# Two-phase convolution for three of the four channel groups, with the constant products at a tile's end taken out, in a fused attention, router and state-space kernel

## The chip, the cores and the metric

One core of a Trainium2 chip runs the whole program. The metric is the device time of one launch in microseconds (us).

## What is computed

The input x has 8 sequences of 512 tokens with 256 numbers each. Four layers run one after the other, each on the layer-normed x and added to it; the reference, cut to what matters here:

```python
x = x + attention(layernorm(x))            # linear attention, 16 heads
x = x + experts(layernorm(x))              # 8 experts, the best one for each token
x = x + state_space(layernorm(x))          # the layer that is changed
x = x + experts(layernorm(x))

# state_space; d_inner 512, d_state 16, 4 taps
xc, z = split(x @ in_proj_w.T)
h = conv(pad(xc, 3 in front), conv_w)      # 512 x 512 channels, 4 taps, causal
u = h + conv_b
dt = clip(sigmoid(u @ dt_w.T + dt_b), 1e-4, 1.0)
Bm, Cm = u @ B_w.T, u @ C_w.T
state = exp(clip(dt * A)) * state + dt * Bm * u + 1e-6    # per token, 16 states per channel
y = sum(state * Cm) + D * u
out = (y * silu(z)) @ out_w.T
```

## The kernel before

All arithmetic is fp32. Each engine has its own program, written out by hand; semaphores join them. The 8 sequences are called tiles here (`b`, or `n` for the one that is prepared).

**The state-space layer** holds over half of the time. It runs 8 tiles, each of 64 slots (`q`): 16 states by 4 groups of 128 channels. In a slot TensorE turns four 128x128 pieces of the scan's input into PSUM (`m_spread`, L1645ff, recorded under the helper's L1300), ScalarE makes the decay (`m_decay`, L745) and a quarter of the input of the next state (`m_input`, L755), and VectorE runs one scan over 512 tokens (`m_scan`, L1197). After four slots GpSimd multiplies the state's four scans by C (`c_product`, L500) and issues a DMA that adds the product to one of two sums (`add_on`, L509). C comes as one broadcast DMA per state from SyncE's queue (L396), two ahead.

**Beside the scans of tile b the next tile is prepared**, and the last one closed. Tables at the top say in which slot each instruction is issued on TensorE (`CONV_AT`, `UT_AT`, `BC_AT`, `DT_AT`, `DTT_AT`, `Z_AT`, `OUT_AT`, `XT_AT`), on ScalarE (`UC_AT`, `UTC_AT`, `TH_AT`, `ZTH_AT`, `XTC_AT`, `SKIP_AT`) and on VectorE (`ADD_AT`, `FINAL_AT`, `UPDATE_AT`, `STAT_AT`, `CLIP_AT`, `WT_AT`, `GATE_AT`). TensorE may be at most three slots ahead of the scans (three PSUM banks), and it does in order what stands in a slot.

**The convolution** (`m_conv`, L1556ff, products at L1567) has the input projection already folded into its taps (`tap`, L1443ff: `tapw[k]` = in_proj times conv tap k, eight products of four parts, L1449, copied out at L618). For each of 4 output groups `o` it adds up 4 taps by 2 halves of the input: 8 products of 128x128 weights by 512 tokens, so 32 a tile. An fp32 product has two matmul records in the trace, a transpose one. `m_uevac` (L699) copies it out and adds the bias, then come the transposes of u (L1575), the B and C product (L1584) and the dt products (L1598).

**In slots 59, 61 and 62** of each of the first seven tiles TensorE also computes a product of constants that nothing reads (`m_spin`, L1695 to L1699, `SPIN_AT`).

**The rows x** of the first four tiles stay in SBUF from the layer's start; the place of the other four holds two of the seven state buffers, and their rows come again from memory in tiles 2 to 5 (`ld_again`, L403 to L409). Rows of a finished tile go out (`store_rows`), and in the last tile four tiles' rows come back into `staged` for the next router (L416 to L425).

**The first expert layer** begins with the router: TensorE turns x and makes logits (`x_turn`, `logits`), VectorE makes the tables (`feed`, L992ff), GpSimd gathers the rows. TensorE's `feed` places tap product 0 before the counting products L1464 and L1466, 1 and 2 behind them, 3 behind the sorting products L1475; 4 to 7 follow the experts. The tap weights are loaded by SyncE after all rows are stored (L367 to L376).

**Before the first scan** tile 0 is prepared with nothing beside it: TensorE L1725 to L1748, ScalarE norms, copies, three decays and the four input pieces of state 0, VectorE row statistics of all rows, then clips (L1121) and weights (L1134) in the slot order of the tables.

```python
            for o in range(KI):
                for i in range(TAPS * KD):
                    m_conv(0, o, i)
                    if o and i == TAPS:
                        m_uturn(0, o - 1)
                        m_bcmm(0, o - 1)
```

Of the kernel before, what the change touches and what calls it, by code (L numbers as in the profile page):

```python
# [17 lines left out]
P = 128  # L18
BATCH, SEQ, D = 8, 512, 256
TOK = BATCH * SEQ  # L20
NCH = TOK // P
# [12 lines left out]
PAD = TAPS - 1  # L34
LN_EPS, NORM_EPS = 1e-5, 1e-6
# [15 lines left out]
CONV_AT = ((0, 1, 2, 2, 3, 4, 5, 6), (7, 8, 8, 10, 11, 12, 13, 14), (14, 15, 16, 17, 18, 20, 21, 21), (22, 23, 24, 26, 28, 29, 30, 30))  # L51
UT_AT = (12, 19, 25, 34)
OUT_AT = ((23, 25, 25, 26, 28, 29, 32, 33), (38, 39, 41, 43, 43, 47, 49, 49))
BC_AT = (19, 23, 27, 34)
DT_AT = ((33, 34, 36, 36), (37, 38, 39, 40), (43, 44, 45, 47), (48, 49, 50, 51))
DTT_AT = (40, 44, 50, 55)
BT_AT = 41
C_STORE = 10
SPIN_AT = (59, 61, 62)
Z_AT = ((52, 53), (54, 55), (56, 57), (58, 59))  # L60
XT_AT = (52, 53, 55, 57)

# [12 lines left out]
UPDATE_AT = (34, 50)
STAT_AT = (36, 38, 58, 63)
SKIP_AT = (3, 5, 8, 16)
CLIP_AT = (38, 42, 48, 52)
WT_AT = (40, 45, 51, 56)
BTC_AT = 44  # L80
GATE_AT = (55, 57, 59, 61)


XT_BANK, CONV_BANK, UT_BANK, OUT_BANK = (0, 7), (0, 1, 0, 1), (0, 1, 0, 1), (4, 5)
BC_BANK, BT_BANK, DT_BANK, DTT_BANK, Z_BANK, Y_BANK = 7, 7, (0, 1, 0, 1), (0, 1, 0, 1), (4, 5, 4, 5), (4, 5, 7, 4)
SCAN_BANK = (2, 3, 6)
DT_FIRST = (2, 3, 4, 5)

# [55 lines left out]
def build(nc, T):  # L144
    with ExitStack() as ctx:
# [42 lines left out]
        class Space:  # L188
# [5 lines left out]
            def take(self, n):  # L194
# [31 lines left out]
        zero_row = s.take(ROW)  # L226

# [43 lines left out]
                for c in (RING * CPB, (RING + 2) * CPB)]  # L271
        m_c = [s.take(SEQ) for _ in range(RC)]
# [6 lines left out]
                  for w in (m_dt[0].rearrange("p k t -> p (k t)"), u_raw[0]) for i in range(2)]  # L279
        x_turned = ([f_xt[i % 2] for i in range(BATCH)], [halves[i // IN_LAST][i % 2] for i in range(BATCH)])  # L280
# [13 lines left out]
        def kept(b):  # L294

            return CPB * (b % RING)
# [9 lines left out]
        def z_bank(b, o):  # L306
            return ps[(Z_LAST if b == BATCH - 1 else Z_BANK)[o]]

# [16 lines left out]
        def _(sp):  # L325
# [44 lines left out]
            def send_tap(k):  # L370
                if k >= 2:
                    sp.wait_ge(S("tap_mm"), KD * (k - 1))
                sp.dma_start(cw[k % 2], T["conv"][k].rearrange("(k p) d -> p k d", p=P)).then_inc(S(f"ld_cw{k}"), 16)

            for k in range(TAPS - 1):
                send_tap(k)  # L376
# [1460 lines left out]
```

## Time and profile before

| | |
|---|---|
| median of 3 runs | 1475.5 us (1467.76, 1475.50, 1475.68) |
| the profiled execution | 1471.08 us, span 1469.3 us |
| attention and first router, up to the experts | about 0 to 242 us |
| first experts, up to the first preparation | about 242 to 408 us |
| preparation of tile 0 | about 408 to 472 us |
| the 8 tiles of scans | 472.3 to 1263.0 us |
| second router and experts | to 1469.3 us |
| mean granted TensorE clock | 0.978 of full speed |

A duration of a matmul record overlaps the next one's: what one costs in a dense run is the run's length over its count. A row of the timeline merges neighbours of one kind; its bracket is the idle time of that engine before it and what ended it. In a table by stretches each engine's column is its busy time, then the count of records; the clock is the share of full speed, 1.00 being 2.4 GHz and 0.50 being 1.2 GHz.

### The profile page before, as it was taken

How to read it: one execution, taken by the hardware profiler on the slowest of the kernel's cores; microseconds unless marked ns; L12 is line 12 of the kernel's file. 1: busy time of each engine (PE TensorE's matmuls, PEld its weight loads, DVE VectorE, ACT ScalarE, POOL GpSimd, SP SyncE). 2: the span in 40 equal slices, each digit the busy share in tenths (PEclk: the TensorE clock that was granted, in tenths of full speed). 3: DMA queues.
4: the chain of work that ended last, by engine and by line, in shares of the span. 5: the costliest groups of instructions: out<-in, count | busy, mean ns of one | idle time of the engine just before them, and what ended most of it. 6: DMA issues, size and time to landing. Idle time of an engine off the chain costs nothing.

```text
span 1469.3 us, 22230 instructions
## 1 busy us (share of the span) xinstructions
PE 1366.5 (93%) x7040; PEld 949.6 (65%) x7040; DVE 1011.8 (69%) x1529; ACT 937.7 (64%) x1737; POOL 861.1 (59%) x436
## 2 busy tenths in 40 slices
PE   5899998999998999999999999999999887979997
PEld 2566686999744555565655655655656576569996
DVE  6666634333332899899899898998998988853332
ACT  1222231344314999899999998999999999214442
POOL 1111002555200899798898897998988979225552
PEclk9999989999998999999999999999999979999999
DMA  9200044777420598898997997988979979376662
GB/s 301 85 29 29 19 98 144 211 206 210 153 65 16 118 219 195 179 221 186 201 222 181 205 220 176 218 190 193 223 170 204 230 195 234 79 235 203 208 210 82
DMA packets 108229, 248.39 MB, mean 169 GB/s; under 512 B 19097, under 2 KB 49950, under 8 KB 94048
## 3 DMA queue, kind: packets, MB, share of 16 engines
q0 software_dynamic: 23104, 131.96, 41.5%
q1 hardware_dynamic: 82944, 113.68, 25.6%
q10 hardware_dynamic: 2080, 1.47, 0.3%
q8 instruction: 55, 0.90, 0.2%
q14 instruction: 46, 0.38, 0.1%
HBM read 116.72 MB, written 18.94 MB: 92 GB/s over the span
## 4 chain that ended last, share of the span: by engine, by line
PE 67%; ACT 16%; DVE 10%; issue 4%; DMA 1%; another core or an unknown queue 1%; SPq 0%; DVEq 0%; ACTq 0%; POOLq 0%; POOL 0%
PE ps L1300 11%; PE ps L1513 9%; PE ps L1504 9%; PE ps L1567 7%; ACT arena L745 7%; PE ps L1598 7%; ACT arena L755 7%; PE ps L1325 4%; PE ps L1640 3%; PE ps L1629 3%; DVE arena L1197 3%; PE ps L1362 2%; PE ps L1584 2%; PE ps L1316 2%; PE ps L1449 1%
## 5 line engine op out<-in xcount | busy, mean ns | idle before, releaser
L500 POOL TENSOR_TENSOR arena<-arena 128x2048 f32<-128x2048 f32 x91 | 425.1, 4684 | 118.6 <-DVE arena L1197 117.4
L1300 PEld LDWEIGHTS ps<-cst,arena 128*128 128x128 f32 x2428 | 295.3, 143 | 280.1 <-issue 187.7
L1197 DVE TENSOR_TENSOR_SCAN arena<-arena,ps 128x512 f32<-128x512 f32 x364 | 431.7, 1209 | 62.3 <-PE ps L1300 58.7
L1300 PE MATMUL ps<-cst,arena 128*128 128x128 f32 x2428 | 365.7, 278 | 51.2 <-ACT arena L755 24.3
L745 ACT ACTIVATE arena<-arena,a_neg 128x512 f32<-128x512 f32 x512 | 365.9, 715 | 43.3 <-DVE arena L1197 29.6
L755 ACT ACTIVATE arena<-arena,m_bt 128x512 f32<-128x512 f32 x512 | 362.9, 709 | 3.8 <-DVE arena L1134 2.2
L1567 PE MATMUL ps<-arena,tapw 128*128 128x512 f32 x512 | 255.1, 600 | 0.7 <-ACT arena L693 0.7
L1197 DVE TENSOR_TENSOR_SCAN x<-arena,ps 128x512 f32<-128x512 f32 x148 | 175.7, 1209 | 21.9 <-PE ps L1300 20.6
L500 POOL TENSOR_TENSOR x<-x,arena 128x2048 f32<-128x2048 f32 x36 | 169.8, 4728 | 14.7 <-DVE x L1197 12.7
L1078 DVE TENSOR_TENSOR arena<-ps,arena 128x256 f32<-128x256 f32 x78 | 33.1, 425 | 205.7 <-PE ps L1513 131.4
L456 POOL DMA_INDIRECT arena<-rows,arena x78 | 75.9, 973 | 158.1 <-DVE arena L1058 134.9
L1504 PEld LDWEIGHTS ps<-arena 128*128 128x128 f32 x1248 | 154.7, 196 | 3.8
L1504 PE MATMUL ps<-arena 128*128 128x128 f32 x1248 | 154.9, 279 | 0.0
L1513 PE MATMUL ps<-arena 128*128 x624 | 147.5, 380 | 3.3 <-ACT arena L644 3.3
L637 ACT ACTIVATE arena<-ps 128x256 f32<-128x256 f32 x78 | 30.0, 385 | 157.8 <-PE ps L1300 156.5
L1598 PE MATMUL ps<-arena,dtw 128*128 128x512 f32 x256 | 128.6, 597 | 0.6 <-ACT arena L699 0.6
L1513 PEld LDWEIGHTS ps<-arena 128*128 128x128 f32 x624 | 112.5, 190 | 16.0 <-issue 3.7
L644 ACT ACTIVATE arena<-ps,b1t 128x128 f32<-128x128 f32 x312 | 89.3, 370 | 43.8 <-issue 29.5
L1567 PEld LDWEIGHTS ps<-arena,tapw 128*128 128x128 f32 x512 | 85.1, 193 | 36.1 <-issue 33.7
L447 POOL TENSOR_TENSOR x<-x,arena 128x1024 f32 (+1 forms) x8 | 18.9, 2358 | 120.0 <-DVE arena L868 114.4
L471 POOL DMA_INDIRECT residual<-arena x39 | 39.4, 1011 | 68.4 <-DVE arena L1085 67.2
L471 POOL DMA_INDIRECT out_x<-arena x39 | 39.3, 1008 | 67.5 <-DVE arena L1085 67.5
(164 smaller groups left out, 1573.0 us busy)
## 6 DMA issues: line engine op xcount, KB each, us to landing
arena<-arena POOLq DMA_DIRECT2D x52, 1024.0 KB, 8.3
arena<-in_W SPq DMA_DIRECT2D x94, 512.0 KB, 8.2
arena<-c_rows SPq DMA_DIRECT2D x128, 256.0 KB, 3.7
arena<-x POOLq DMA_DIRECT2D x28, 1024.0 KB, 8.4
x<-arena POOLq DMA_DIRECT2D x24, 1024.0 KB, 8.3
rows<-x SPq DMA_DIRECT2D x16, 512.0 KB, 4.2
x<-residual SPq DMA_DIRECT2D x12, 512.0 KB, 5.9
x<-in_x SPq DMA_DIRECT2D x8, 512.0 KB, 11.2
```

The costliest lines, as they stand in the source:

```text
L456: g.indirect_dma_start(out=t_x[j % XB], out_offset=None, in_=xs[r], in_offset=bass.IndirectOffsetOnAxis(ap=idx[:, j:j + 1], axis=0))\
L471: g.indirect_dma_start(out=x_mid if r == 0 else T["out"].rearrange("b s d -> (b s) d"), out_offset=bass.IndirectOffsetOnAxis(ap=idx[:, j:j ...
L500: g.tensor_tensor(h, h, m_c[i % RC].unsqueeze(1).to_broadcast([P, KI, SEQ]), ALU.mult)\
L644: last = a.activation(t_ht[par][:, k, :], ps[4 + par][:, k * P:(k + 1) * P], ACT.Relu, bias=b1t[:, row(e), k:k + 1].rearrange("p a b -> p ...
L745: a.activation(m_a[g % RA], m_dt[b % 2][:, k, :], ACT.Exp, scale=a_neg[:, k, n:n + 1])\
L755: a.activation(m_dbt[i % 2][:, c, :], m_wt[b % 2][:, c, :], ACT.Copy, bias=1e-6, scale=m_bt[b % 2][:, c, n:n + 1]).then_inc(S("m_dbt"), 1)
L1197: v.tensor_tensor_scan(out=h[:, k, :], data0=m_a[g % RA], data1=ps[SCAN_BANK[g % 3]][:, :], initial=0.0, op0=ALU.mult, op1=ALU.add).then_i ...
L1300: return t.transpose(bank, src[:, k * P:(k + 1) * P], ident)
L1504: last = t.matmul(ps[4 + par][:, h * P:(h + 1) * P], t_w1[j % WR][:, k, h * P:(h + 1) * P], t_xt[par][:, k, :], start=(k == 0), stop=(k == ...
L1513: last = t.matmul(ps[6 + par][:, 0:D], t_ht[par][:, k, :], w2[:, row(e), k, :].rearrange("p a h -> p (a h)"), start=(k == 0), stop=(k == K ...
L1567: mm = t.matmul(ps[CONV_BANK[o]][:, :], tapw[:, k, d, o * P:(o + 1) * P], m_xt[n % 2][:, d, k:k + SEQ], start=(i == 0), stop=(i == TAPS * ...
L1598: mm = t.matmul(dt_bank(n, o)[:, :], dtw[:, k, o * P:(o + 1) * P], m_u[n % 2][:, k, :], start=(k == 0), stop=(k == KI - 1))
```

## The change

**The convolution in two phases.** Even and odd tokens are computed together, from products over half the tokens each, with three quarters of the columns of before. Phase one (part 0) multiplies sums of two neighbouring taps (`tap_sum`, `sum_first`) with every second token: four products of 256 tokens, in one half of a shared bank (`BOTH_BANK`). ScalarE adds the bias and writes them into every second column of u (`m_both`). Phase two (parts 1 and 2) multiplies single taps with differences of neighbouring tokens (`m_xd`, `xd_first`): eight products of 256 or 255 tokens. VectorE adds both (`m_join`). GpSimd makes the sums of taps once and the two differences once a tile (`m_differ`, after product 15). Groups 1 to 3 of tiles 1 to 7 are done so, and all four groups of tile 0; group 0 of the others stays as it was. All slot tables are changed.

**The constant products** `m_spin` and `SPIN_AT` are gone.

**Rows.** `m_xd` and `tap_sum` take the place of rows in SBUF, so rows of each tile are loaded twice: for its norm (at n == 8) and for its update (at n == 2); at the end of tile 6 three loads stand together. The rows of tiles 4 and 5 come back into the taps' place.

**Before the first scan** clips and weights are in another order, VectorE makes two of the four input pieces of state 0, and two norms and turns of tile 1 come earlier. **In the first router** the tap weights are loaded at the program's start, tap product 0 stands between the logits, 1 before the counting products, 2 behind them and 3 between the sorting products.

```diff
-CONV_AT = ((0, 1, 2, 2, 3, 4, 5, 6), (7, 8, 8, 10, 11, 12, 13, 14), ...
-SPIN_AT = (59, 61, 62)
+CONV_AT = ((0, 1, 1, 2, 3, 4, 5, 6), (5, 6, 7, 7, 9, 9, 10, 10, 11, 11, 12, 13), ...
+JOIN_AT = (15, 20, 24)
...
+                    if n == N_LOAD and b < BATCH - 2:
+                        sp.wait_ge(S("m_umm"), conv_done(b + 1, KI - 1))
+                        if b:
+                            sp.wait_ge(S("ld_rows"), 16 * b)
+                        sp.dma_start(x[:, CPB:2 * CPB, :],
...
+            def m_differ(n):
+                g.wait_ge(S("m_xtc"), KD * (n + 1))
+                for s in range(2):
+                    g.tensor_tensor((m_xd if n else xd_first)[:, s], m_xt[n % 2][:, :, PAD + 1 - 2 * s:PAD + SEQ - 2 * s:2],
+                                    m_xt[n % 2][:, :, PAD:PAD + SEQ - 1:2], ALU.subtract).then_inc(S("m_xd"), 1)
...
+            def m_both(n, o):
+                a.wait_ge(S("m_umm"), conv_done(n, o, BOTH_END))
...
+                a.activation(m_u[n % 2][:, o, 1::2], both_bank(n)[:, o % 2 * HALF:(o % 2 + 1) * HALF], ACT.Identity,
+                             bias=mvec[:, 0, o:o + 1]).then_inc(S("m_both"), 1)
...
+            def m_join(n, o):
+                v.wait_ge(S("m_both"), both_done(n, o))
...
+                v.wait_ge(S("m_umm"), conv_done(n, o))
+                u = m_u[n % 2][:, o, :].rearrange("p (t s) -> p t s", s=2)
+                v.tensor_tensor(u, ps[CONV_BANK[o]][:, :].rearrange("p (s t) -> p t s", s=2),
+                                u[:, :, 1].unsqueeze(2).to_broadcast([P, HALF, 2]), ALU.add).then_inc(S("m_u"), 1)
...
+                if part == 0:
+                    out, lo = both_bank(n), o % 2 * HALF
+                    w = (tap_sum if n else sum_first)[:, j, d, o * P:(o + 1) * P]
+                    mm = t.matmul(out[:, lo:lo + HALF], w, m_xt[n % 2][:, d, PAD - 2 * j:PAD - 2 * j + SEQ - 1:2],
+                                  start=first, stop=last)
+                else:
+                    out, lo = ps[CONV_BANK[o]], (2 - part) * HALF
+                    w = tapw[:, TAPS - part - 2 * j, d, o * P:(o + 1) * P]
+                    mm = t.matmul(out[:, lo + j:lo + HALF], w, (m_xd if n else xd_first)[:, part - 1, d, 0:HALF - j], start=first, stop=last)
...
-            def m_spin(b, q):
...
-                t.matmul(ps[DTT_BANK[KI - 1]][:, :], ones, cst[:, 0:4 * P], start=True, stop=True)
```

TensorE at the joint of two tiles, slots 60 to 65 of the kernel before. A row is an instruction; L1300 are the scan's transposes into banks 2, 3 and 6, L1699 the constant product, L1567 the convolution's first products for the tile after.

```order
L1699 MATMUL ps1<-cst 128x512 [waits m_wt]
L1300 MATMUL ps2<-cst,arena 128x128 [waits m_scan,m_dbt]
L1300 MATMUL ps2<-cst,arena 128x128 x3
L1300 MATMUL ps3<-cst,arena 128x128 [waits m_scan]
L1300 MATMUL ps3<-cst,arena 128x128 x3
L1699 MATMUL ps1<-cst 128x512
L1300 MATMUL ps6<-cst,arena 128x128 [waits m_scan]
L1300 MATMUL ps6<-cst,arena 128x128 x3
L1699 MATMUL ps1<-cst 128x512
L1300 MATMUL ps2<-cst,arena 128x128 [waits m_scan]
L1300 MATMUL ps2<-cst,arena 128x128 x3
L1300 MATMUL ps3<-cst,arena 128x128 [waits m_scan,m_dbt]
```

The same place in the changed kernel, where L1778 is the gate's product, L1422 a transpose (into banks 7 and 0 those of the tile after the next), L1693 the convolution:

```order
L1778 MATMUL ps5<-arena,zw 128x512
L1422 MATMUL ps7<-cst,arena 128x128 [waits m_xn]
L1422 MATMUL ps0<-cst,arena 128x128
L1422 MATMUL ps2<-cst,arena 128x128 [waits m_scan,m_dbt]
L1422 MATMUL ps2<-cst,arena 128x128 x3
L1422 MATMUL ps3<-cst,arena 128x128 [waits m_scan]
L1422 MATMUL ps3<-cst,arena 128x128 x3
L1422 MATMUL ps6<-cst,arena 128x128 [waits m_scan]
L1422 MATMUL ps6<-cst,arena 128x128 x3
L1422 MATMUL ps2<-cst,arena 128x128 [waits m_scan]
L1422 MATMUL ps2<-cst,arena 128x128 x3
L1422 MATMUL ps3<-cst,arena 128x128 [waits m_scan,m_dbt]
```

Between the gate's last product and the convolution's first only the scan's transposes are left.

TensorE at the end of the preparation of tile 0, before: L1598 are the dt products, L1613 the transposes of dt, L1300 the turns of tile 1 (banks 0 and 7) and then of the first slot (bank 2).

```order
L1613 MATMUL ps2<-cst,arena 128x128 [waits m_dt1]
L1613 MATMUL ps2<-cst,arena 128x128 x3
L1598 MATMUL ps5<-arena,dtw 128x512 [waits m_u] x4
L1613 MATMUL ps3<-cst,arena 128x128 [waits m_dt1]
L1613 MATMUL ps3<-cst,arena 128x128 x3
L1613 MATMUL ps4<-cst,arena 128x128 [waits m_dt1]
L1613 MATMUL ps4<-cst,arena 128x128 x3
L1613 MATMUL ps5<-cst,arena 128x128 [waits m_dt1]
L1613 MATMUL ps5<-cst,arena 128x128 x3
```

And in the changed kernel, where L1747 are the dt products and L1762 the transposes of dt:

```order
L1747 MATMUL ps5<-arena,dtw 128x512 [waits m_u] x2
L1762 MATMUL ps3<-cst,arena 128x128 [waits m_dt1]
L1762 MATMUL ps3<-cst,arena 128x128 x3
L1747 MATMUL ps5<-arena,dtw 128x512 [waits m_u] x2
L1762 MATMUL ps4<-cst,arena 128x128 [waits m_dt1]
L1762 MATMUL ps4<-cst,arena 128x128 x3
L1422 MATMUL ps7<-cst,arena 128x128 [waits m_btc,m_utc,m_xn]
L1422 MATMUL ps0<-cst,arena 128x128
L1422 MATMUL ps7<-cst,arena 128x128 [waits m_xn]
L1422 MATMUL ps0<-cst,arena 128x128
L1762 MATMUL ps5<-cst,arena 128x128 [waits m_dt1]
L1762 MATMUL ps5<-cst,arena 128x128 x3
```

The transpose of dt for group 1 now stands between the last dt products, and half of tile 1's turns ahead of the last transpose of dt.

## Rows read from the trace of the kernel before

**Rows 1.** Tile 2 by stretches of 8 slots (first, second, last), and all eight summed.

```profile
core 0: us, PE busy (x) PEld busy (x) DVE busy (x) ACT busy (x) POOL busy (x), PEclk, DMA share, GB/s
667.60:678.50 10.90, 10.85 (x50) 6.17 (x48) 10.03 (x11) 10.90 (x19) 10.54 (x5) 1.00 1.01 220
678.50:692.50 14.00, 13.32 (x62) 7.79 (x61) 13.79 (x18) 13.61 (x23) 11.33 (x5) 1.00 0.59 149
...
754.50:767.20 12.70, 11.18 (x52) 6.53 (x53) 12.13 (x15) 12.00 (x21) 12.20 (x6) 1.00 1.01 215
sum 99.60, PE 96.42 PEld 58.67 DVE 90.85 ACT 93.35 POOL 87.23; mean PE 12.05 PEld 7.33 DVE 11.36 ACT 11.67 POOL 10.90
```

**Rows 2.** Dense runs on TensorE, timeline: start us, us, engine, line, operation.

```profile
191.68 3.70 PE L1362 MATMUL ps<-arena 128*128 128x256 f32 x16
433.75 7.14 PE L1567 MATMUL ps<-arena,tapw 128*128 128x512 f32 x16
```

**Rows 3.** What one instruction costs on VectorE and on ScalarE, timeline of each.

```profile
664.42 0.66 DVE L1139 SCALAR_TENSOR_TENSOR arena<-arena,ps 128x512 f32<-128x512 f32 x1
665.00 2.32 DVE L1197 TENSOR_TENSOR_SCAN arena<-arena,ps 128x512 f32<-128x512 f32 x2
```

```profile
763.10 0.72 ACT L745 ACTIVATE arena<-arena,a_neg 128x512 f32<-128x512 f32 x1 [0.31 <-DVE x L1197]
763.73 0.71 ACT L755 ACTIVATE arena<-arena,m_bt 128x512 f32<-128x512 f32 x1
```

**Rows 4.** The joint of tiles 2 and 3, timeline of TensorE.

```profile
760.29 1.02 PE L1699 MATMUL ps<-cst 128*128 128x512 f32 x2
761.15 1.03 PE L1300 MATMUL ps<-cst,arena 128*128 128x128 f32 x8
...
765.72 0.66 PE L1300 MATMUL ps<-cst,arena 128*128 128x128 f32 x4 [0.94 <-ACT arena L755]
766.21 1.02 PE L1567 MATMUL ps<-arena,tapw 128*128 128x512 f32 x2
```

**Rows 5.** Where the clock fell and rose, table by stretches, columns as in rows 1.

```profile
463.00:466.00 3.00, 1.43 (x8) 1.20 (x9) 1.42 (x3) 1.71 (x3) 0.00 (x0) 0.88 0.00 0
...
472.00:475.00 3.00, 3.00 (x9) 1.81 (x8) 1.22 (x1) 3.00 (x6) 0.00 (x0) 0.50 0.00 0
475.00:478.00 3.00, 3.00 (x10) 1.40 (x10) 2.44 (x2) 2.58 (x5) 0.00 (x0) 0.91 0.00 0
...
1193.00:1196.00 3.00, 0.89 (x6) 0.59 (x6) 3.00 (x5) 2.62 (x6) 2.56 (x2) 0.96 0.69 150
1205.00:1208.00 3.00, 3.00 (x20) 2.64 (x19) 2.52 (x3) 2.56 (x4) 3.00 (x1) 0.84 1.14 295
```

**Rows 6.** The preparation of tile 0, timelines of ScalarE, TensorE and VectorE.

```profile
410.96 12.96 PE L1567 MATMUL ps<-arena,tapw 128*128 128x512 f32 x26 [0.69 <-ACT arena L693]
456.92 0.43 PE L1606 MATMUL ps<-cst,arena 32*128 32x32 f32 x4
466.35 0.69 DVE L1134 SCALAR_TENSOR_TENSOR arena<-ps,arena 128x512 f32<-128x512 f32 x1 [1.19 <-PE ps L1613]
467.08 2.56 ACT L755 ACTIVATE arena<-arena,m_bt 128x512 f32<-128x512 f32 x4 [2.21 <-DVE arena L1134]
469.54 1.07 ACT L686 ACTIVATE arena<-x,nw,scales 128x256 f32<-128x256 f32 x2
472.25 1.22 DVE L1197 TENSOR_TENSOR_SCAN arena<-arena,ps 128x512 f32<-128x512 f32 x1 [5.21 <-PE ps L1300]
```

**Rows 7.** The first router, timelines of TensorE and VectorE.

```profile
215.38 5.73 PE L1449 MATMUL ps<-arena 128*128 128x512 f32 x8 [1.75 <-DMA arena<-in_conv]
221.65 0.42 DVE L1016 TENSOR_REDUCE arena<-ps 128x8 f32<-128x256 f32 x1 [3.35 <-PE ps L1464]
```

**Rows 8.** A product of GpSimd at a joint, timeline; its DMAs and the row loads, DMA issues.

```profile
668.24 4.87 POOL L500 TENSOR_TENSOR arena<-arena 128x2048 f32<-128x2048 f32 x1
```

```profile
arena<-arena POOLq DMA_DIRECT2D x52, 1024.0 KB, 8.3
x<-residual SPq DMA_DIRECT2D x12, 512.0 KB, 5.9
```

More of the change, by code:

```diff
@@ L279, in build @@
                   for w in (m_dt[0].rearrange("p k t -> p (k t)"), u_raw[0]) for i in range(2)]
+        staged += [tapw[:, k].rearrange("p d n -> p (d n)").rearrange("p (c d) -> p c d", c=CPB) for k in range(2)]
         x_turned = ([f_xt[i % 2] for i in range(BATCH)], [halves[i // IN_LAST][i % 2] for i in range(BATCH)])
@@ L368, in _ @@
             sp.wait_ge(S("row_zeroed"), 32)
-            sp.dma_start(ipw, T["ip_x"].rearrange("(k p) d -> p k d", p=P)).then_inc(S("ld_cw0"), 16)
[L370 to L376, printed above, removed]
+            send_tap(2)
             send_w1(0)
@@ L1410, in x_turn @@
                     for k in range(KD):
-                        rows = staged[b][:, c, :] if r and b < RING else x[:, (kept(b) if r else CPB * b) + c, :]
+                        rows = staged[b][:, c, :] if r and b < BATCH - 2 else x[:, (kept(b) if r else CPB * b) + c, :]
                         last = turned(ps[FEED_PAIR[r][i][k]][:, c * P:(c + 1) * P], rows, k, c)
@@ L1467, in feed @@
                 if r == 0:
-                    for n in range(1, 3):
-                        tap(n // KD, n % KD)
+                    tap(2)
                 else:
@@ L1562, in m_conv @@
+                part, (d, j) = i // len(TURN_OF), TURN_OF[i % len(TURN_OF)]
+                first, last = i % len(TURN_OF) == 0, (i + 1) % len(TURN_OF) == 0
+                if o == (1 if n else 0) and i == 0:
+                    t.wait_ge(S("m_zero"), 6 if n else 4)
+                    t.wait_ge(S("m_xtc"), KD * (n + 1))
+                if o == (1 if n else 0) and part and first:
+                    t.wait_ge(S("m_xd"), 2 * n + part)
                 if o == 1 and i == 0 and n >= 2:
                     t.wait_ge(S("m_wt"), KI * n)
-                if o >= 2 and i == 0:
+                if o and i == 0:
+                    t.wait_ge(S("m_both"), both_done(n, o) - 1)
@@ L1658, in m_prep @@
                 for o in range(KI):
-                    for i in range(TAPS * KD):
+                    for i in range(len(CONV_AT[o])):
                         if q == CONV_AT[o][i]:
@@ L1725, in _ @@
             for o in range(KI):
-                for i in range(TAPS * KD):
+                for i in range(PARTS):
                     m_conv(0, o, i)
-                    if o and i == TAPS:
+                    if o and i == PARTS // 2:
                         m_uturn(0, o - 1)
@@ L1743, in _ @@
                 m_dtmm(0, 3, k)
-            for o in range(1, KI):
-                m_dturn(0, o)
-            for c in range(CPB):
+                if k == 1:
+                    m_dturn(0, 1)
+            m_dturn(0, 2)
+            for c in range(XN):
+                m_turn(1, c)
+            m_dturn(0, 3)
+            for c in range(XN, CPB):
                 m_turn(1, c)
```

298 lines of the change are left out of this document (194 added, 104 removed).

## The prediction

> **What bounds the kernel now.** I read the table of busy time by stretches first, because the change rearranges work on all engines and a share of the whole span says little. Over one tile of 99.6 us TensorE is busy for 96.4 us, ScalarE for 93.4, VectorE for 90.9 and GpSimd for 87.2 [rows 1]. No engine bounds the tile alone. In its first eight slots ScalarE and TensorE are busy to the full 10.9 us, in the next eight VectorE leads (13.8 of 14.0). So work taken from one engine is paid back only where that engine leads.
>
> Then I read unit costs, since busy times of matmuls overlap. An fp32 product has two records: 16 records of 256 columns stand in 3.70 us, so such a product costs about 0.43 to 0.46 us; a constant product of 512 columns begins 0.86 us before what follows it, and eight transposes begin 0.87 us before the next, so four cost 0.44 [rows 2, 4]. Sixteen records of 512 columns take 7.14 us, or 0.86 to 0.89 a product [rows 2]. VectorE's scan takes 1.1 to 1.2 us and one small operation of 512 columns about 0.6; ScalarE's decay and input take 0.6 us each, so ScalarE needs 1.2 us of every slot too [rows 3]. (A row's own length includes its tail; the spacing of starts is what counts.)
>
> Third, the clock, table by stretches. At the joint of two tiles it stays 1.00 [rows 1], and there the constant products stand between the transposes [rows 4]. It fell elsewhere: in 463 to 466 it averaged 0.88 while TensorE was busy for 1.43 of 3 us, and it was still 0.50 in 472 to 475 although TensorE was busy for all 3.00; in the next 3 us it averaged 0.91 [rows 5]. Read as halves of full speed, it fell near 465.3 and rose near 475.5, so it was at 1.2 GHz for 10.2 us, some 3.5 of them in saturated work. In the last tile it began to fall with 0.89 us of matmul in 3 us, and later averaged 0.84 in a stretch that was saturated throughout [rows 5].
>
> **The change part by part, against the profiled execution's 1471.1 us.** That run lies 4 us under the median of 1475.5, and the three runs spread from 1467.8 to 1475.7; I put the forecast 1 us above the sum for this.
>
> *Inside a tile.* Group 0 of the convolution keeps its 8 products; in groups 1 to 3, 24 products of 0.86 us (20.6) become 36 of 0.43 (15.5), so 5.2 us less on TensorE. Three constant products of 0.86 are another 2.6 less. VectorE gets three joins at 0.6, so +1.8. ScalarE's copies of u shrink by about 0.2 each. I laid the slot tables out in groups of eight slots and added unit costs. Before, the leading engine of each group needs 11.2, 13.7, 13.1, 12.1, 12.6, 10.9, 12.7 and 12.5 us, together 98.8, against 99.6 measured [rows 1], so the layout is good to a per cent. After: 12.1, 13.1, 12.5, 11.9, 11.6, 12.1, 11.3 and 12.5, together 97.1. TensorE alone falls from 93.9 to 86.1, but it wins little of this: in most groups VectorE or ScalarE is right behind. In the first group it even loses: eight full products, four of the half ones and 32 transposes are 6.9 + 1.7 + 3.5 = 12.1 us, where it had 11.2. That is 1.7 us gained a tile. I take 1.4, because GpSimd's two differences (512 columns of 2048; a product of 2048 takes 4.87 us [rows 8], so 1.2 us each) stand between its product 15 and the eight products of phase two that read them, and GpSimd has only 12.4 us of room a tile. Seven tiles: **-9.8 us**. If the layout's gain is hidden entirely it is 0; if every stretch follows TensorE it could be 3 a tile, -21.
>
> *Strided operands.* Phase one reads every second token. No row shows a matmul with such an operand. The bounds are 0.43 (as 256 contiguous columns [rows 2]) and 0.86 (as if all 512 passed) for 12 products a tile, so 0 to 5.2 us on TensorE; I take 0.43, the row with the same number of columns. The joins and `m_both` are strided as well: 0.6 to twice that, up to 1.8 on VectorE, taken as 0.6. The Trainium skill's "SBUF — State Buffer", section "Door 1: The DMA port swizzle", says that two hits in a line of 16 bytes suffice for full bandwidth; fp32 at a stride of two makes two, so by that page the stride costs nothing; no row here shows it.
>
> *The clock at the joints.* Without the constant products, from the gate's last product to the convolution's first only 16 transposes remain, 1.7 us of TensorE in four slots of over 1.2 us each, some 5 to 7 us. That is sparser than 1.43 in 3 us, where it fell [rows 5]. What follows is the first group, where TensorE now leads with 12.1 us, so a slow clock is paid in time. From the two recoveries in rows 5 saturated work runs at half speed for 1.0 to 3.5 us before the clock rises, and the end of a spell may already slow the transposes: I take 4.2 us at half speed, so 2.1 us lost a joint. Six joints lie ahead of a tile with a full convolution behind it; at 0.85 each: 6 x 2.1 x 0.85 = **+10.7 us**. From below 0 (it holds), from above 6 x 5.1 = 31 (a spell of 10.2 us, all of it saturated). The Trainium skill, "TensorE: Matmul & The Clock Gate", section "Loop structure matters more than you think", says matmuls kept back to back stay at full speed and a long wait between them halves it. By that rule read strictly, a joint without a long wait would keep its clock; the longest idle time there is 0.94 us [rows 4]. The first fall in rows 5 speaks against so strict a reading, and it gives the first rival.
>
> *Preparation of tile 0.* TensorE is saturated there from 410.96 on [rows 2, 6]. 32 products of 0.86 are 27.5 us, 48 of 0.43 are 20.6, so -6.9; the first waits for both copies of x instead of one, +0.5: **-6.4 us**. If the stride costs double, its 16 products take back 6.9.
>
> *End of that preparation.* From the transposes at 456.92 to the first scan at 472.25 nothing but latency counts: the last dt weight at 466.35, four input pieces on ScalarE in 2.56 us, two norms of tile 1 (1.07), the turns, then the scan after 5.21 us of idle time [rows 6]. Afterwards the transposes of dt stand between the last dt products, which brings the last weight forward by some 2.7 us; VectorE makes two of the four pieces, which halves 2.56, -1.3; and norms and turns of tile 1 are done ahead, -1.4. **-5.4 us**, between -2 and -7.
>
> *First router.* Tap product 0 waits for its weights until 215.38 and VectorE waits 3.35 us for the counting product queued behind it [rows 7]. Loaded at the program's start the wait of 1.75 goes, but the product now stands ahead of the last logits, 3.4 us of them: **-1.0**, between -3 and +1.
>
> *Row loads.* One more load of 512 KB a tile (5.9 us from issue to landing) beside GpSimd's adds of 1024 KB (8.3 us) [rows 8]; the DMA engines' share is already about 1.0 in the first and last eight slots [rows 1]. Loads are issued slots ahead, so nothing is late in most tiles; at the end of tile 6 three stand together, **+1**, between 0 and 3.
>
> Sum: 1471.1 - 9.8 + 10.7 - 6.4 - 5.4 - 1.0 + 1.0 = 1460.2; with the offset to the median **1461 us**. A measurement of this kernel can tell about 1% (14.8 us) from no change, so under 1460.7 counts as faster: the forecast stands on this line.
>
> **The rivals.**
>
> *The clock holds at the joints.* For it: the longest idle time there is under 1 us, and transposes do run. Against it: rows 5. Then the 10.7 falls away: 1450 us. Chance 0.2.
>
> *The joints go cold for long, and it ends slower.* If each fall lasts 10.2 us as at 465 [rows 5] and all of it lies in saturated work, a joint loses 5.1 us, six lose 31, and 1471.1 - 21.6 + 31 = 1480.5, say 1480. The point from which it decides: the other terms sum to -21.6, so at 3.6 us lost a joint there is no gain left. Against it: much of the 10.2 was latency, not saturated work. Chance 0.1.
>
> *The tiles gain nothing.* GpSimd's differences come late or strided products cost double; TensorE then waits in or after slot 9, or the joins delay the scans. For it: GpSimd is busy for 87 of 99.6 us and trails the scans. Then -9.8 becomes 0, with the clock's cost kept: 1470.5. Chance 0.17. A milder form is that the three short edits (preparation, its end, router) do less than they say; that moves it by 5 at most.
>
> *My forecast,* 1461, own range 1455 to 1467: chance 0.53.
>
> **How the numbers follow.** The range of 8 in 10 takes in the first rival's 1450 with a few us below it, and reaches to half of the slow one: 1445 to 1476. Faster by over 1% holds the first rival (0.2) and a little under half of the forecast (0.26): 0.46. Slower by over 1% means over 1490, which the slow rival reaches only with its spread: 0.06. The rest, 0.48, is within 1%.
>
> **What would show it right or wrong.** The table by stretches should show the clock below 1.00 at the starts of tiles 1 to 6 and at full speed within the first eight slots; tiles of about 99.6 - 1.4 + 1.8 = 100.0 us, with the first eight slots longer than 10.9 and the others shorter. If the clock is 1.00 there, tiles take 98.2. Dense products of phase one should be spaced 0.43 us; 0.86 would mean the stride costs. The first scan should come about 49 us after the first preparation product (61.3 - 6.9 - 5.4), where it was 61.3 [rows 6]; VectorE's wait for the counting product should be gone. A long wait of TensorE for GpSimd's differences, or of VectorE for the joins' products, would make the forecast wrong, as would a fall of the clock in mid-tile, where TensorE now has 8 us less to do.

## The result and the profile after

The changed kernel takes 1489.7 us (median of 4 runs, 1487.5 to 1491.6) against 1474.4 for the kernel before: a ratio of 1.011, 95% interval 1.008 to 1.014. It is slower; 1461 was forecast. The profiled execution took 1491.5 us, span 1489.7, so 20.4 us more span than before. Here and below, medians and ranges are of the executions in the fast state; one of run 6 and one of run 8 were slow and are left out. Where the 20.4 us are:

| stretch | before | after | difference | forecast |
|---|---|---|---|---|
| start to first scan | 472.3 | 465.8 | -6.4 | -12.8 |
| tiles 0 to 6 | 693.1 | 698.7 | +5.6 | +0.9 |
| tile 7 | 97.6 | 118.6 | +21.0 | +1 |
| behind the last scan | 206.3 | 206.6 | +0.3 | 0 |

Tile 2 by stretches of 8 slots, which answers to [rows 1]:

```profile
core 0: us, PE busy (x) PEld busy (x) DVE busy (x) ACT busy (x) POOL busy (x), PEclk, DMA share, GB/s
657.40:675.20 17.80, 15.74 (x64) 9.34 (x63) 10.74 (x10) 11.61 (x19) 15.93 (x7) 0.88 0.95 211
675.20:688.70 13.50, 12.21 (x65) 9.89 (x64) 13.28 (x17) 12.92 (x23) 12.99 (x5) 0.88 0.53 127
...
748.70:760.60 11.90, 8.02 (x43) 4.97 (x42) 11.90 (x16) 11.90 (x21) 11.60 (x6) 0.99 1.05 245
sum 103.20, PE 93.74 PEld 64.15 DVE 92.24 ACT 92.46 POOL 89.59; mean PE 11.72 PEld 8.02 DVE 11.53 ACT 11.56 POOL 11.20
```

(Tile 0 alone gained 3.8 us, so the six tiles behind a joint, 1 to 6, are 9.4 longer together.) The first 8 slots take 17.8 us where they took 10.9; the last are shorter, 11.9 for 12.7. (TensorE's busy sum is inflated by the low clock.) The gain on the arithmetic is there and is lost again at the joint. What VectorE does in those 8 slots:

```profile
659.94 1.22 DVE L1296 TENSOR_TENSOR_SCAN arena<-arena,ps 128x512 f32<-128x512 f32 x1 [1.34 <-PE ps L1422]
662.86 5.11 DVE L1296 TENSOR_TENSOR_SCAN arena<-arena,ps 128x512 f32<-128x512 f32 x4 [1.70 <-PE ps L1422]
671.76 0.70 DVE L1244 TENSOR_TENSOR ps<-ps,x 128x512 f32<-128x512 f32 x1 [3.79 <-DMA x<-x]
```

Two waits for TensorE, which runs at the low clock up to about 661 (table below), and then 3.79 us for a DMA. L1244 is the first add of the finished tile's even sum, and the DMA is the last one that GpSimd adds to that sum. Before, the same add never waited in any tile; it stood in slot 7, and now stands in slot 5. The clock at this joint:

```profile
653.00:656.00 3.00, 0.49 (x4) 0.25 (x3) 3.00 (x5) 3.00 (x6) 2.60 (x2) 0.75 1.05 223
656.00:659.00 3.00, 2.77 (x7) 1.64 (x8) 2.57 (x3) 3.00 (x6) 0.79 (x2) 0.50 1.01 231
659.00:662.00 3.00, 3.00 (x9) 1.71 (x8) 1.22 (x1) 2.26 (x5) 3.00 (x1) 0.61 1.06 225
662.00:665.00 3.00, 3.00 (x15) 1.72 (x14) 2.06 (x2) 1.42 (x3) 2.70 (x3) 1.00 0.59 139
```

It fell to 1.2 GHz (0.50), as forecast, for about 7 us; at four of the other five joints it was about 3.4 us. In tiles 2, 3 and 6 it fell a second time, for 3.4 us from the end of the first 8 slots on (0.88 in the second row of the table by stretches). GpSimd is late too. In tile 1, ahead of this joint, it stands still ahead of the first norm (L574) until the store of C has landed; SyncE issued that store at 616.70 (timelines of GpSimd and SyncE, then the table of waits over the tiles):

```profile
625.63 0.55 POOL L574 TENSOR_SCALAR arena<-x,scales,nw 128x256 f32<-128x256 f32 x1 [4.87 <-DMA c_rows<-arena]
```

```profile
616.70 0.32 SPq L431 DMA_DIRECT2D c_rows<-arena  x1
```

```profile
POOL arena L574 <- DMA c_rows<-arena: 21.5, 6, 5.3
```

21.5 us in six waits; before there were none. In the changed tables the norm stands behind product 8, not 9 (`NORM_AFTER`), but the store moved forward by one as well (`C_STORE`, 10 to 9). What differs is how long the store takes from issue to landing, here of all eight stores of C, before and after:

```profile
DMA to landing us min/median/max: 1.6/3.3/4.2
DMA to landing us min/median/max: 1.6/6.8/9.3
```

In tiles 0 to 5 that is 3.2 to 4.2 us before and 6.1 to 9.3 after. The new row load at n == 8 now stands ahead of the store in SyncE's queue, 6.7 to 8.4 us earlier; before there was no load there:

```profile
608.28 0.55 SPq L456 DMA_DIRECT2D x<-residual  x1
```

That this load is what slows the store was not tried.

The last tile (timelines of TensorE, VectorE, GpSimd and SyncE):

```profile
1176.85 1.97 PE L1422 MATMUL ps<-cst,tapw 128*128 128x128 f32 x8 [10.80 <-DMA tapw<-rows]
```

```profile
1179.71 3.44 DVE L1296 TENSOR_TENSOR_SCAN arena<-arena,ps 128x512 f32<-128x512 f32 x3 [11.75 <-PE ps L1422]
```

```profile
1178.96 4.54 POOL L581 TENSOR_TENSOR arena<-arena 128x2048 f32<-128x2048 f32 x1 [13.91 <-DMA arena<-c_rows]
```

```profile
1148.77 0.37 SPq L392 DMA_DIRECT2D rows<-x  x1
1151.81 0.32 SPq L440 DMA_DIRECT2D arena<-c_rows  x1
1157.29 1.80 SPq L463 DMA_DIRECT2D tapw<-rows  x2
1159.13 1.57 SPq L466 DMA_DIRECT2D x<-residual  x1
1160.74 23.10 SPq L440 DMA_DIRECT2D arena<-c_rows  x3
```

SyncE does in order what stands in its program. At the end of tile 6 it stores tile 5's rows, waits until 1157.29 for them to land, issues three row loads, and only then the next broadcasts of C. The router's first turn reads the first of these loads (`tapw<-rows`), but waits for one semaphore that counts two: the first landed after 7.7 us, the second after 19.1, at 1176.8. It stands on TensorE ahead of the scan's transposes, so everything stops for 11 us; GpSimd waits 13.9 us for the broadcast behind the loads.

### The profile page after: what moved, and what is told of

It is laid out like the page before. It is cut to its first block, busy times and chain, and to the rows that moved or that the text cites. A ratio compares the mean times of both kernels' runs of the same rounds, so it can differ in the third digit from the quotient of the medians.

```text
span 1489.7 us, 22662 instructions
## 1 busy us (share of the span) xinstructions
PE 1342.5 (90%) x7198; PEld 1003.7 (67%) x7198; DVE 1026.1 (69%) x1556; ACT 929.7 (62%) x1735; POOL 886.2 (59%) x456
## 4 chain that ended last, share of the span: by engine, by line
PE 58%; issue 10%; DVE 9%; POOL 7%; DMA 7%; ACT 7%; SPq 0%; DVEq 0%; POOLq 0%; ACTq 0%
PE ps L1635 9%; PE ps L1422 9%; PE ps L1644 9%; PE ps L1747 4%; PE ps L1447 4%; DVE arena L1296 3%; PE ps L1719 3%; POOL arena L581 3%; ACT arena L830 3%; DMA arena<-arena 2%; ACT arena L840 2%; PE ps L1789 2%; PE ps L1484 2%; PE ps L1733 2%; PE ps L1553 2%
## 5 line engine op out<-in xcount | busy, mean ns | idle before, releaser
L1422 PEld LDWEIGHTS ps<-cst,arena 128*128 128x128 f32 x2428 | 301.5, 147 | 259.5 <-issue 136.8
L1422 PE MATMUL ps<-cst,arena 128*128 128x128 f32 x2428 | 378.2, 285 | 95.2 <-ACT arena L840 46.1
L581 POOL TENSOR_TENSOR arena<-arena 128x2048 f32<-128x2048 f32 x91 | 431.8, 4759 | 54.0 <-DVE arena L1296 37.0
L1747 PE MATMUL ps<-arena,dtw 128*128 128x512 f32 x256 | 125.6, 593 | 0.0
L1644 PEld LDWEIGHTS ps<-arena 128*128 128x128 f32 x624 | 112.6, 190 | 12.2
L1719 PE MATMUL ps<-x,tapw 128*128 128x256 f32 (+1 forms) x336 | 90.5, 390 | 0.0
L1693 PE MATMUL ps<-arena,tapw 128*128 128x512 f32 x112 | 65.7, 683 | 0.0
```

The costliest lines, as they stand in the source:

```text
L581: g.tensor_tensor(h, h, m_c[i % RC].unsqueeze(1).to_broadcast([P, KI, SEQ]), ALU.mult)\
L1422: return t.transpose(bank, src[:, k * P:(k + 1) * P], ident)
L1644: last = t.matmul(ps[6 + par][:, 0:D], t_ht[par][:, k, :], w2[:, row(e), k, :].rearrange("p a h -> p (a h)"), start=(k == 0), stop=(k == K ...
L1719: mm = t.matmul(out[:, lo + j:lo + HALF], w, (m_xd if n else xd_first)[:, part - 1, d, 0:HALF - j], start=first, stop=last)
L1747: mm = t.matmul(dt_bank(n, o)[:, :], dtw[:, k, o * P:(o + 1) * P], m_u[n % 2][:, k, :], start=(k == 0), stop=(k == KI - 1))
```

## Experiments

Each is against the kernel before on the same chip. Medians are of 4 to 10 runs, ranges in brackets, and ratios with their intervals are to the kernel before on that chip, whose medians were 1469.3 (runs 1 to 4), 1472.8 (5 to 8) and 1472.5 (9 to 12). Between runs of different numbers the ratios are the safer comparison: 0.1 of a per cent is 1.5 us.

**1. The constant products back.**

```diff
+SPIN_AT = (59, 61, 62)
...
+                        if q in SPIN_AT:
+                            m_spin(b, q)
```

> The changed kernel with the three constant products of a tile put back in slots 59, 61 and 62, nothing else. My theory: the clock at the joints is one of three causes, worth 2 to 3 us at each of six joints, so 1475 to 1480 us; the granted clock is 1.00 at the starts of tiles 1 to 6; TensorE's wait of 10.8 us for the rows at the start of the last tile stays, and that tile stays above 110 us. Rival (the missing products are the whole cause, the last tile's 21 us included): 1455 us or less, last tile 98 us.

Measured: 1491.2 us (1484.3 to 1496.1), ratio 1.0136 (1.0076 to 1.0196). Both expected times were missed: nothing came back. TensorE's wait for the rows stayed, as expected (10.5 us, last tile 118.1). The clock is whole at the start of each of tiles 1 to 6, here in the first (561 to 564 us of this run, with the stretch after it); in tiles 2, 3, 5 and 6 it fell only later, near the end of the first 8 slots:

```profile
561.00:564.00 3.00, 3.00 (x14) 1.78 (x13) 2.85 (x3) 3.00 (x6) 2.79 (x1) 1.00 1.06 221
564.00:567.00 3.00, 3.00 (x17) 2.19 (x16) 0.53 (x2) 2.13 (x4) 2.91 (x4) 1.00 1.04 225
```

The first 8 slots still take 14.5 to 17.9 us. What TensorE gained, VectorE waited for the sum's DMA; the table of waits has 19.7 + 4.9 + 3.8 = 28.4 us in six joints for that add, against 14.1 in five in the changed kernel:

```profile
DVE ps L1245 <- DMA arena<-arena: 19.7, 4, 6.5
DVE ps L1245 <- DMA x<-x: 4.9, 1, 4.9
DVE ps L1245 <- DMA arena<-x: 3.8, 1, 3.8
```

This overthrew my first account (clock plus a few misplaced loads) and gave the second: two limits one behind the other, the clock and the chain of adds.

**2. The kernel before without its products.**

```diff
-                        if q in SPIN_AT:
-                            m_spin(b, q)
```

> The kernel before with its constant products taken out and nothing else. My theory: its clock falls at the joints as in the changed kernel, and since TensorE leads in the first eight slots there too, six or seven joints lose 2 us each: 1484 us (1480 to 1488), first eight slots 13 us where they were 10.9, last tile within 2 us of 97.6. Rival: the convolution of full products keeps the clock up by itself, or ScalarE leads and hides it: 1474 us, as before.

Measured: 1478.1 us (1467.3 to 1487.3), 1.0057 (1.0022 to 1.0092). This lies under the range I expected, and the last tile took 101.1 us, more than the expected 2 us from 97.6. By the medians the products are worth 8.8 us there. The traces put only part of it at the joints: tiles 1 to 6 are 2.8 us longer together, the last tile 3.5, with a lower clock in it. The clock does not fall at each joint. In the profiled execution it held at two of the six, and one can see both cases in neighbouring tiles, the first 8 slots of tile 2 and of tile 3:

```profile
669.40:681.90 12.50, 12.50 (x52) 7.08 (x51) 10.30 (x11) 11.55 (x20) 11.61 (x6) 0.93 1.01 218
```

```profile
769.80:780.80 11.00, 10.95 (x50) 6.28 (x49) 10.11 (x11) 11.00 (x19) 10.41 (x5) 1.00 1.02 222
```

With the fall 12.5 us, without it 11.0: 1.5 us a fall, where I had 2.1.

**3. The norm one product later.**

```diff
-NORM_AFTER = (8, 10, 11, 12)
+NORM_AFTER = (9, 10, 11, 12)
```

> The changed kernel with GpSimd's first norm of a tile behind its product 9, where it was before, not behind product 8. My theory: the wait of 4.9 us for the store of C in tiles 1, 2 and 5 goes, GpSimd ends its tile 5 slots behind the scans rather than 7, and the first eight slots of tiles 2, 3 and 6 take 14.5 us rather than 17.8, 17.3 and 16.9: 1481 us (1479 to 1484). Rival: these three joints are slow for another reason (DMA, clock), and the time stays at 1490.

Measured: 1482.1 us (1475.5 to 1494.6), 1.0082 (1.0047 to 1.0117). That is 7.6 us under the changed kernel by the medians, 4 by the ratios, whose intervals overlap; it is the trace that shows the effect. The wait for the store is gone from the table of waits (the store still takes 6.2 to 9.3 us); GpSimd waits 10.4 us for broadcasts of C instead. Tiles 2, 3 and 6 begin with 14.2, 15.0 and 15.6 us. These joints were longer than the others because GpSimd was late.

**4. The row loads apart.**

```diff
+                    if n == N_LOAD and b == BATCH - 2:
...
+                        sp.dma_start(staged[RING], xs[1][RING * SEQ:(RING + 1) * SEQ, 0:D].rearrange("(c p) d -> p c d", p=P))\
+                            .then_inc(S("ld_early"), 16)
...
+                    if n == 8 and b == BATCH - 1:
+                        sp.wait_ge(S("ld_rows"), 16 * (BATCH - 2))
```

> The changed kernel, but of the three row loads that stand together at the end of tile 6 one is issued at product 8 of tile 6 (tile 4's rows) and one at product 8 of tile 7 (tile 7's rows), and the router's first turn waits for tile 4's rows alone. My theory: TensorE's wait of 10.8 us and GpSimd's of 13.9 us for the C broadcast at the start of the last tile go; that tile takes 104 to 108 us instead of 118.6: 1477 us (1473 to 1481). Rival (the last tile is long because the clock is low in it): still 115 us or more, 1487 to 1490.

Measured: 1484.6 us (1471.3 to 1489.9), 1.0086 (1.0055 to 1.0118), again within reach of the changed kernel's interval and above the 1473 to 1481 expected; last tile 109.6 for 118.6, where I had 104 to 108. TensorE's wait for the rows is gone; GpSimd's stays at 9.0 us, since the broadcast still stands behind SyncE's wait for the store of tile 5's rows:

```profile
1168.69 4.51 POOL L585 TENSOR_TENSOR arena<-arena 128x2048 f32<-128x2048 f32 x1 [9.01 <-DMA arena<-c_rows]
```

**5. The adds later.**

```diff
-ADD_AT = ((5, 6, 13, 16), (11, 12, 15, 17))
+ADD_AT = ((7, 8, 13, 16), (11, 12, 15, 17))
```

> The changed kernel with VectorE's first two adds of a tile's even sum in slots 7 and 8, where they were before, not in 5 and 6. Since putting the constant products back (the first experiment) brought nothing, my second theory is that the first eight slots end with the DMA that closes the last tile's sum: VectorE waits for it in slot 5 (0.9 to 3.8 us in the changed kernel), and a faster TensorE only waits longer. Then here that wait goes, the first eight slots of tiles 1 to 6 take 13 us (with the low clock at the joints as the next limit) where they took 14.3 to 17.8, and the time is 1480 us (1476 to 1484). Rival (the low clock ends these slots): no change, 1488 to 1491.

Measured: 1481.8 us (1475.6 to 1484.6), 1.0063 (1.0043 to 1.0083). The add's waits fall from 14.1 us to 0.4:

```profile
DVE ps L1244 <- DMA arena<-arena: 0.4, 1, 0.4
```

The first 8 slots take 13.4 to 15.0 us, 14.2 on average, a us more than I had; the last tile is still 115.9.

**6. Adds later and the products back** (edits of 1 and 5).

> As the run before, with the constant products put back too. My second theory: now TensorE's clock is the last limit, so the products bring what they bring in the kernel before (9 us there): first eight slots 12.3 us, 1472 us (1467 to 1476); last tile still above 112. Rival (the products bring nothing in this arrangement, wherever the adds stand): the same as the run before within 3 us.

Measured: 1477.9 us (1473.9 to 1485.9), 1.0047 (1.0022 to 1.0072). Only 4 us less than run 5 (2 by the ratios), which is near the rival's outcome; the add waited again, for 4.8 us in three joints, while GpSimd was still late from its wait for C's store. Where it did not wait, the first 8 slots took 12.2 us.

**7. Norm and row loads.** Edit 3 and edit 4, with tile 5's load moved on:

```diff
-                    if n == NS - 2 and b == BATCH - 2:
+                    if n == 0 and b == BATCH - 1:
                        sp.wait_ge(S("f1_rows"), 16 * (BATCH - 2))
```

> The changed kernel with GpSimd's norm behind product 9 (third experiment) and the row loads apart (fourth), tile 5's load moved on behind the first C broadcast of tile 7, so that no C broadcast stands behind the wait for the store of tile 5's rows. My theory: in the fourth run GpSimd still waited 9.0 us for that broadcast and VectorE 6.4 us for the sum behind it; both go, the last tile takes 102 to 106 us, and with the norm's part the time is 1470 us (1465 to 1475). Rival (the low clock of the last tile is what is left): last tile 109 as in the fourth run, 1478 or more.

Measured: 1469.2 us (1460.6 to 1482.2), 0.9968 (0.9935 to 1.0000); last tile 104.8. Against run 3 the loads alone are 1.1 points of the ratio, 17 us (13 by the medians), of which the last tile shows 11.9 (116.7 there). The low clock is not what made the last tile 118.6 us long: it is at 0.73 in its first 8 slots here (0.65 in the changed kernel), which now take 15.1 us, not 22.1. Before they took 12.1 at 0.91, so some of the last 3 us may be the clock's. In tiles 0 to 6 GpSimd waits 19.1 us for broadcasts of C in this run, and tile 1 takes 102.3.

```profile
1157.30:1172.40 15.10, 9.83 (x60) 8.15 (x58) 10.29 (x11) 12.04 (x21) 11.44 (x5) 0.73 1.04 238
```

**8. All four together.**

> All four together: adds in slots 7 and 8, constant products back, norm behind product 9, row loads apart. My theory: the causes add up, tiles 1 to 6 take 97 to 98 us, the last 102 to 105, first scan near 465: 1455 us (1450 to 1460), faster than the kernel before. Rival (the two-phase arrangement is bound by GpSimd's or the DMA engines' work and not by these waits): 1466 or more.

Measured: 1461.1 us (1455.3 to 1467.8), 0.9916 (0.9893 to 0.9940). Faster than before by 0.8%, and a little above the 1450 to 1460 expected. Tiles 2 to 6 take 97.9 to 98.0 us, the last 103.3; tile 1 takes 100.4. (In the profiled execution the first router ran at half clock from 201 us on, which made its first scan 10 us late; the median does not hang on it.) Tile 2, by stretches:

```profile
667.40:679.70 12.30, 12.30 (x61) 7.98 (x60) 10.23 (x11) 12.29 (x21) 11.71 (x7) 1.00 1.04 232
679.70:693.50 13.80, 11.37 (x68) 9.22 (x67) 13.77 (x18) 12.50 (x22) 13.27 (x5) 1.00 0.54 144
...
sum 98.00, PE 91.73 PEld 63.41 DVE 92.22 ACT 92.72 POOL 88.07; mean PE 11.47 PEld 7.93 DVE 11.53 ACT 11.59 POOL 11.01
```

**9. As run 8, without the products.**

> The eighth run's kernel without the constant products (adds in slots 7 and 8, norm behind product 9, row loads apart). My theory: with the other waits gone the low clock shows by itself; first eight slots of tiles 1 to 6 take 13.4 to 14 us where they took 12.2, tiles 99.3 instead of 97.9, and the time is 1471 us (1467 to 1475) against 1461 there. Rival (the products bring nothing in the two-phase arrangement): within 3 us of 1461.

Measured: 1469.3 us (1464.7 to 1474.2), 0.9971 (0.9951 to 0.9991). So once these waits are gone the products are worth 8 us by the medians and by the ratios, whose intervals leave some 4 to 13; tiles 1 to 6 are 9.3 us longer together than in run 8. The first 8 slots of tiles 1 to 6 take 13.4 to 15.0 us, 14.1 on average, against 12.2 in tiles 2 to 6 of run 8. The first 8 slots of tile 4 (856.4 to 870.2), with TensorE busy throughout:

```profile
856.40:870.20 13.80, 13.80 (x61) 8.65 (x61) 10.28 (x10) 12.30 (x21) 12.93 (x7) 0.92 1.00 224
```

Runs 7 and 9 differ by the adds alone and take the same time within their intervals. So with norm and loads mended but without the products the adds' place costs nothing that can be told, and with early adds (run 1) the products bring nothing: the two limits stand near one height. (Run 1 also has the early norm; early adds and products with norm and loads mended were not tried.) In the profiles the first 16 slots of the least disturbed tiles take 14.3 + 13.2 = 27.5 us with early adds and no products (the changed kernel's tile 4), 14.5 + 13.2 = 27.7 with the products alone (tile 1 of run 1), 13.8 + 13.8 = 27.6 with later adds alone, and 12.2 + 13.8 = 26.0 when both are mended. Single tiles scatter: tile 4 of run 3, with neither, took 13.4 + 13.2 = 26.6 at a clock of 0.92.

**10. The kernel before with early adds.**

```diff
-ADD_AT = ((7, 8, 10, 15), (12, 14, 14, 17))
+ADD_AT = ((5, 6, 10, 15), (12, 14, 14, 17))
```

> The kernel before with its first two even adds moved from slots 7 and 8 to 5 and 6, nothing else. My theory of the adds: VectorE waits 1 to 3 us in slot 5 for the DMA that closes the last sum, with full clock and full products; first eight slots of tiles 1 to 6 at least 12.5 us where they were 10.9, of which the next eight give half back; 1481 us (1477 to 1486). Rival (the wait only hurts where the two-phase products or the low clock have made TensorE late): no change, 1470 to 1475.

Measured: 1479.2 us (1473.0 to 1480.8), 1.0048 (1.0031 to 1.0064). With full products and full clock the early adds cost 6.7 us. The first 8 slots of tile 2 take 12.7 us, not 10.9, the next 13.5, not 14.0:

```profile
672.29 0.70 DVE L1147 TENSOR_TENSOR ps<-ps,x 128x512 f32<-128x512 f32 x1 [1.45 <-DMA x<-x]
```

**11. Tap product 3 behind the sorting products.**

```diff
-                    if r == 0:
-                        tap_part(3, i)
...
                 if r == 0:
+                    tap(3)
                     t.wait_ge(S("tapw"), KD * 2)
```

> The changed kernel with tap product 3 of the first router behind the sorting products, where it was before, not between them. My theory of the router's missed gain: each piece of 0.9 us stands ahead of the next sorting products on TensorE, so the first expert's first product starts 2 to 3 us earlier here, near 245 us in a run whose clock in the router is as in the changed kernel's; the whole time 1487 us, which the timing may not tell. Rival (VectorE's sorting ends this stretch): the product starts as late as before.

Measured: 1492.6 us (1489.8 to 1496.8), 1.0144 (1.0119 to 1.0170); first expert product at 246.7 us, against 247.3 in the changed kernel. The rival's outcome, but for a reason that neither had: here the 64 records of sorting products run at half clock, 13.15 us long, and eat what was saved. In run 12, also without the tap's pieces among them, 48 of the 64 did so. Why is not shown: in the kernel before they stand without pieces too, and took 8.9 us at full clock. TensorE's timeline and the stretch:

```profile
227.25 13.15 PE L1605 MATMUL ps<-arena 128*128 128x80 f32 x64 [2.87 <-DVE arena L1134]
```

```profile
232.00:236.00 4.00, 4.00 (x21) 4.00 (x20) 3.04 (x4) 0.00 (x0) 0.00 (x0) 0.50 0.00 0
```

**12. All four, with tap product 3 behind** (edits of 8 and 11).

> The eighth run's kernel (all four) with tap product 3 behind the sorting products. My theory: 2 us less than there, 1459 us (1455 to 1463), the fastest of all, faster than the kernel before by 0.8 to 1 per cent. Rival: the same as the eighth run.

Measured: 1459.9 us (1457.3 to 1463.0), 0.9909 (0.9886 to 0.9932). The fastest median, but not to be told from run 8's. The last tile took 107.8 us here.

## Why the prediction was wrong

The sign was wrong. The sum came to 1460.2 for the profiled execution, which took 1491.5: 31 us missed. The table at the top splits them into 20 in the last tile, 5 in the others and 6 before the first scan.

**The step that failed most is "Row loads".** It priced the three loads at the end of tile 6 at 1 us, between 0 and 3, by the reasoning that loads are issued slots ahead. I had looked at the DMA engines' time alone, and not at SyncE's order: the loads stand behind a wait for a store and ahead of broadcasts of C, and the router's turn, which before read rows that lay in SBUF, became a wait on TensorE ahead of the scans, for two loads where it reads one. For SyncE's waits the sum named nothing that is queued behind them. Moving these loads took 9.0 us out of the last tile (run 4), and 11.9 against run 3 once a broadcast no longer stood behind the wait for the store (run 7). "Nothing is late in most tiles" failed too: the store of C, behind the new load at n == 8, landed 6.1 to 9.3 us after its issue, not 3.2 to 4.2. The last tile is still 103 to 108 us in runs 7, 8, 9 and 12, where 97.6 stood before. In it GpSimd waits for broadcasts of C for 8.2, 14.2 and 4.8 us in runs 7 to 9, where it waited 0.8 before; what holds those 6 to 10 us was not tried and stays open.

**The second is "Inside a tile".** It counted work by 8 slots and had no place for the waits that came with two small moves in the tables. The adds went from slots 7 and 8 to 5 and 6, ahead of the DMA that they read; the norm went one product forward, together with a store of C that now lands later. Neither stands in my sum, and runs 3, 5 and 10 show what they cost: by the ratios 4, 7 and (in the kernel before) 7 us. They overlap, as both end in the same place: a late GpSimd makes the last sum late. (The intervals of runs 3 and 5 touch the changed kernel's; it is the waits in the traces that show the effect.) My bounds went by GpSimd's room, 12.4 us a tile, and a queue can be late with room to spare. The count of work itself held: with all four mended tiles 2 to 6 take 97.9 to 98.0 us, and 98.2 had been forecast for a whole clock.

**The clock was the mechanism it was said to be, and near its size.** It fell at the joints and rose within the first 8 slots. Forecast 10.7 us; measured 8, with intervals that leave 4 to 13 (run 9 against 8), and 9.3 by tiles 1 to 6 in the traces of these two. A joint lost 1.9 us there, where 2.1 was taken. In the kernel before a fall cost less, 1.5 us. The second falls, in tiles 2, 3 and 6, come near the fall in mid-tile that the prediction named as a sign against it. But in this change the clock was no separate term: run 1 shows that without it the time stays, since the adds waited for their DMA for longer (28.4 us for 14.1). A sum of costs was the wrong form; two limits of one stretch are a maximum.

**Strided operands cost next to nothing,** as taken. In the preparation four products that read every second token stand in 1.82 us (435.22 to 437.04), three of contiguous columns behind them in 1.29 (to 438.33): 0.455 and 0.43 each. A join took 0.67 us on VectorE, as its other operations of 512 columns did. The Trainium skill's "SBUF — State Buffer", section "Door 1: The DMA port swizzle", had it so for the operand in SBUF.

```profile
435.22 1.98 PE L1714 MATMUL ps<-arena 128*128 128x256 f32 x8
437.04 1.45 PE L1719 MATMUL ps<-arena,tapw 128*128 128x256 f32 x6
438.33 0.60 PE L1726 MATMUL ps<-cst,arena 128*128 128x128 f32 x4
```

**Before the first scan** 12.8 us were forecast and 6.4 came. The router gave +2.0 instead of -1.0 in the profiled execution (the preparation's first product after the taps at 409.73, before at 407.73). That is within the spread: with the same program up to there, runs 1, 3 to 7 and 9 have it at 405.1 to 411.4, and runs 2 and 10, with the kernel before's, at 410.9 and 403.9. So no gain of the router is seen and no loss either. The preparation began 0.6 later after that, as forecast, and gave 5.4 of 6.9, in part because its first products ran at half clock after the gap in front of them: eight records in 3.75 us, where 1.98 is the rule.

```profile
413.55 3.75 PE L1714 MATMUL ps<-arena 128*128 128x256 f32 x8 [1.27 <-ACT arena L774]
```

Its end gave 3.6 of 5.4: 2.0 of the 2.7 up to the last weight, and 1.6 of the 2.7 behind it. The rest of the second part lies in a step that the sum did not have. VectorE takes a branch (L1393, before L1271) ahead of the scans, and the first wait behind it (L1291, before L1192) ends 2.8 us after the branch. Each of the two, before and then after:

```profile
L1271 DVEq COMPARE_BRANCH  x1: 67/67/67, 467.0 to 467.0; - x1
L1192 DVEq EVENT_SEMAPHORE  x405: 21/21/21, 469.9 to 1259.7; - x135
L1393 DVEq COMPARE_BRANCH  x1: 67/67/67, 462.9 to 462.9; - x1
L1291 DVEq EVENT_SEMAPHORE  x405: 21/21/21, 465.8 to 1279.8; - x135
465.82 1.22 DVE L1296 TENSOR_TENSOR_SCAN arena<-arena,ps 128x512 f32<-128x512 f32 x1 [2.71 <-ACT arena L830]
```

Before, the transposes that the first scan reads ended at 472.2, behind all this, and the scan began at once. In the changed kernel they ended at 464.7, and the scan still came at 465.82, 1.1 us later. The decay that the profile names in the bracket is the fourth; the first scan reads the first one, which was done at 455.5.

**The rivals.** The one on the slow side named the place, the joints, and said 1480 with a low clock of 10 us; the clock was low for less, and a wait for DMAs did the rest. "The tiles gain nothing" was near in its cause (GpSimd late) and had no last tile. The range ended at 1476 because every bound in it was one of work or of clock, and none was of a queue.

## What to carry to other kernels

When a table of slots changes, list for each moved instruction what it waits for and when that lands, in the trace of before, and set the new slot beside it: an add moved two slots forward costs nothing in work and all of its DMA's lateness. Ask as well what now stands ahead of that DMA in its queue. A DMA issued behind a wait holds up every DMA behind it in its queue, so price a load by what stands after it there. When two causes end the same stretch, test them one at a time and together; either alone may bring nothing. A single execution's first scan moved by some 6 us between runs of the same program up to there (461.6 to 467.8, and 476.0 in run 8), so terms of 1 or 2 us need several traces.

## What was not expected of the hardware

A TensorE that is busy throughout can stay at 1.2 GHz. In run 11 the sorting products (80 columns) ran for 13 us, from 228 on with TensorE busy for 4.00 of 4 us and the clock at 0.50 (rows under experiment 11). In run 8 the first router's turns, logits (8 columns) and tap product 0 (512 columns) did so from 201 to about 234 us:

```profile
216.00:220.00 4.00, 4.00 (x14) 2.94 (x14) 0.00 (x0) 0.49 (x2) 0.00 (x0) 0.50 0.00 0
```

The Trainium skill's "TensorE: Matmul & The Clock Gate", section "Loop structure matters more than you think", has matmuls kept back to back staying at full speed; these runs show back-to-back records that did not.

Whether the clock falls is not fixed by the program. In run 2 it held at two joints of six that have the same instructions.

Behind VectorE's branch ahead of the first scan 2.8 to 3.0 us pass before the first wait behind it ends, in all 14 traces, though what it waits for was there before.

A load of 512 KB took 7.7 and 19.1 us from issue to landing at the end of tile 6, for the two of one kind, where the DMA engines' share was about 1.0; the median of the row loads before was 5.9 [rows 8].

```profile
DMA to landing us min/median/max: 7.7/13.4/19.1
```
